# Two short attentions of a four-layer kernel: routing moved into the attention's vector loop, early gathers, output projections unrolled by hand, first loads issued in the projections

## What is computed

```python
# layer 0, mixer: two softmax maps a head, 16 heads of 8
heads = jnp.einsum('bhqk,bhkd->bhqd', w0 - lamb * w1, v).transpose(0, 2, 1, 3)
mu = jnp.mean(heads, axis=-1, keepdims=True)
var = jnp.mean((heads - mu) ** 2, axis=-1, keepdims=True)
normed = (heads - mu) * jax.lax.rsqrt(var + EPS) * ln_w[None, None] + ln_b[None, None]
return jnp.einsum('bse,ed->bsd', normed.reshape(b, s, H * DH), wo)
...
# layer 1, mixer: only the queries with the largest (max - mean) score keep their output
sparsity = scores.max(axis=-1) - scores.mean(axis=-1)
_, top_idx = jax.lax.top_k(sparsity, U)
...
return out @ Wo + bo
...
# layer 1, experts: 64 experts in 8 groups, 8 of a token, from its 4 best groups
scores = jax.nn.sigmoid(logits)
sfc = scores + correction_bias[None, :]
top2, _ = jax.lax.top_k(sfc.reshape(T, G, E // G), 2)
_, gidx = jax.lax.top_k(top2.sum(-1), TOPK_GROUP)
masked = jnp.where(emask > 0, sfc, 0.0)
_, tidx = jax.lax.top_k(masked, K)
tw = jnp.take_along_axis(scores, tidx, axis=1)
tw = tw / (tw.sum(-1, keepdims=True) + 1e-20)          # times 2.5
...
# layer 2, experts: 8 experts of bounded capacity; each token adds the rows of its two
final = jnp.zeros((S + 1, d), xf.dtype).at[idx.reshape(-1)].add(out.reshape(-1, d))[:S]
```

## Time and profile before

| | us |
|---|---|
| median of 3 timed runs | 4274.41 (4273.94 to 4274.72) |
| the profiled execution's own time | 4234.75 |
| its span, first to last instruction | 4232.8 |

### The profile page before, as it was taken

How to read it: one execution, slowest core, us unless ns; L and a number is a source line. 1 busy time by engine, 2 the same in 40 slices (tenths; PEclk the granted TensorE clock), 3 DMA queues, 4 the chain that set the end, 5 groups by cost and what they waited for, 6 DMA issues and landing times. The chain is left out here.

```text
span 4232.8 us, 87140 instructions
## 1 busy us (share of the span) xinstructions
PE 3570.5 (84%) x28212; PEld 2179.9 (52%) x28212; DVE 2473.1 (58%) x5731; ACT 2011.8 (48%) x3955; POOL 1264.9 (30%) x1810
## 2 busy tenths in 40 slices
PE   5799999938997699983299996788987399999997
PEld 2344444426774222222177774357986166666664
DVE  5567777651113577764677776725736366666664
ACT  5366666613334377771033335333334356656662
POOL 0111111100001011110077774423546344444440
PEclk9799999958998699996599997877879599999999
DMA  4322222100001321110266660130003433333330
GB/s 119 80 55 57 57 57 55 39 4 16 11 6 35 77 47 45 42 27 4 63 159 162 159 160 25 71 97 23 3 3 69 66 119 114 111 118 119 114 106 26
DMA packets 198213, 287.69 MB, mean 68 GB/s; under 512 B 40830, under 2 KB 155204, under 8 KB 197624
## 3 DMA queue, kind: packets, MB, share of 16 engines
q1 hardware_dynamic: 193852, 275.81, 23.4%
q0 software_dynamic: 4096, 8.40, 1.4%
HBM read 232.91 MB, written 35.84 MB: 63 GB/s over the span
## 5 line engine op out<-in xcount | busy, mean ns | idle before, releaser
L692 ACT ACTIVATE att_E<-att_pX,att_gs 128x512 f32<-128x512 f32 (+3 forms) x1024 | 722.6, 739 | 400.7 <-PE att_pX L625 176.5
L725 DVE TENSOR_REDUCE att_mx<-att_pS 128x1 f32<-128x512 f32 (+4 forms) x960 | 730.1, 787 | 278.2 <-PE att_pS L599 178.7
L1824 POOL TENSOR_TENSOR att_E<-att_E,att_rz 128x128 f32<-128x128 f32 (+3 forms) x512 | 357.6, 719 | 438.1 <-DVE att_rz L2032 438.1
L594 PE MATMUL att_pS<-att_ks,att_qs 72*128 72x512 bf16 (+4 forms) x1536 | 410.5, 339 | 57.8 <-DMA att_ks<-parts 31.8
L1541 POOL TENSOR_TENSOR pairs_h<-pairs_m,pairs_r 128x512 f32<-128x512 f32 x272 | 345.9, 1272 | 351.2 <-DVE pairs_m L1604 349.7
L619 PE MATMUL att_pX<-att_qs,att_ks 75*128 75x512 bf16 (+4 forms) x1536 | 422.0, 330 | 30.3 <-ACT att_E L692 15.4
L1565 PEld LDWEIGHTS pairs_po<-pairs_a,pairs_h 128*128 128x128 f32 x2176 | 285.9, 192 | 129.6 <-issue 129.1
L556 POOL CAST att_mp<-att_m 16x128 bf16<-16x128 f32 x288 | 80.5, 279 | 900.9 <-DVE att_m L736 875.1
L636 PE MATMUL att_pO<-att_E,att_vs 128*9 128x512 f32 (+3 forms) x3072 | 322.0, 491 | 1.3 <-ACT att_E L692 1.3
L1586 ACT ACTIVATE pairs_r<-pairs_ph 128x512 f32<-128x512 f32 x272 | 162.4, 597 | 330.8 <-PE pairs_ph L1557 330.8
L1963 ACT ACTIVATE att_E<-att_S,att_nm 128x128 f32<-128x128 f32 (+3 forms) x512 | 282.1, 556 | 39.8 <-DVE att_nm L2026 39.6
(11 more groups left out here) (416 smaller groups left out, 6576.6 us busy)
## 6 DMA issues: line engine op xcount, KB each, us to landing
pairs_c<-weights SPq DMA_DIRECT2D x272, 256.0 KB, 3.9
att_bias<-in_bias_dram SPq DMA_DIRECT2D x64, 896.0 KB, 4.6
parts<-proj_part SPq DMA_DIRECT2D x144, 128.0 KB, 2.3
att_xb<-xnT SPq DMA_DIRECT2D x64, 256.0 KB, 2.7
att_qs<-parts SPq DMA_DIRECT2D x192, 64.0 KB
att_ks<-parts SPq DMA_DIRECT2D x192, 64.0 KB
att_w<-in_w3a_dram SPq DMA_DIRECT2D x64, 192.0 KB, 2.4
att_qs<-parts SPq DMA_DIRECT2D x96, 96.0 KB
```

What stands on the lines that cost most here:

```text
L594: ins = nc.tensor.matmul(pS[:, bank, n * w:(n + 1) * w], qs[:K1, u, x, q * P:(q + 1) * P], ks[:K1, u, x, :w], start=(n == 0 or not causal) ...
L692: nc.scalar.activation(E[:, kt % 2, WIDE * xp:WIDE * (xp + 1), :w], places(c)[0], ACT.Exp, scale=gs[:, g % 2, gain_of:gain_of + 1]).then_i ...
L725: V.reduce_max(dst, src, AX.X).then_inc(s_mx, 1)
L1824: nc.gpsimd.tensor_tensor(E[:, k, :width(j)], E[:, k, :width(j)], rz[:, u, k:k + 1].broadcast_to([P, width(j)]), ALU.mult).then_inc(s_n, 1)
```

## The change

Five things are different.

1. The attention's query, key, constant, mask and gain buffers move into a class `Arrivals`, opened around projection and attention. The constants are loaded at the head of the projection's SP queue, and the first group's ten loads in the projection's last body, between the puts of its two sequences. The attention's SP queue begins with group 1.
2. `outproj_phase` is written out for eight sequences. In `out0` the mean is folded into the centring, square, root, transposed copy and result are ACT's, and `ln_w`, `ln_b` are applied by ACT as scale and bias of the transposed copy. DVE centres two sequences ahead. In `out1` one instruction masks a sequence. PE transposes a sequence ahead of the product before. Weights are loaded during the norm.
3. `lg_1` runs before `proj1`, with the sigmoid in its last copy. `route` is no phase any more: its DVE work is cut into 24 steps for four tiles, and DVE's loop in `att1` calls one step at every odd `s`, so that 8 steps stand in each of three groups of four, in each of 8 bodies. Each step begins with a drain. `spread` comes after `att1`.
4. 24 of the 64 gathers are issued by POOL in `recur`, behind items 0, 1 and 2 of each body, into new buffers `rows`; `out2` issues 40.
5. ACT and DVE of `out2` weigh the first two quarters among the gates.

```diff
@@ class Arrivals (new), buffers qs, ks, gains, mb and their semaphores
+    def constants(self, sp):
+        for k, dst in enumerate((self.qs, self.ks)):
+            sp.dma_start(dst[STACK:, :].rearrange("r b x t -> r (b x) t"), self.ext[:, k:k + 1].broadcast_to([self.NX + 3, self.NB * self.UN, T])).then_inc(self.s_ce, 16)
...
@@ project_phase, SP
+                arr.constants(sp)
...
+                        if last and g == M2:
+                            for s in s_put:
+                                sp.wait_ge(s, 24 * M2)
+                            arr.load(sp, 0, 0)
...
@@ attend_phase, DVE
                             for c in PLAN[s]:
                                 if not (last and g + 2 >= NB):
                                     extreme(at, g + 2, c)
+                            if aside is not None and s % 2:
+                                aside(dve, i, g * NP2 // 2 + s // 2)
...
@@ outproj_phase, DVE
+                def center(n):
+                    own = heads[:, n * NH * QT:(n + 1) * NH * QT, :]
+                    V.reduce_sum(mu[:, n % 2], own, AX.X)
+                    dve.drain()
+                    V.scalar_tensor_tensor(out=hc[:, n % 4], in0=wide(mu[:, n % 2]), scalar=-1.0 / DH, in1=own, op0=ALU.mult, op1=ALU.add).then_inc(s_c, 1)
...
+                    center(0)
+                    center(1)
+                    for n in range(B):
+                        variance(n)
+                        if n + 2 < B:
+                            center(n + 2)
+                        scale(n)
...
@@ outproj_phase, PE
+                turn(0)
+                for n in range(B):
+                    if n + 1 < B:
+                        turn(n + 1)
+                    project(n)
...
@@ routing
-    CH = 8
+    CH = 4
...
+        def step(dve, i, k):
+            if k > 23:
+                return
+            dve.drain()
...
+            elif k == 7:
+                V.tensor_tensor(gt[:, :, :, :], each(gs[:, :, :]), other(gs[:, :, :]), ALU.is_gt)
+                V.tensor_tensor(eq[:, :, :, :], each(gs[:, :, :]), other(gs[:, :, :]), ALU.is_equal)
...
@@ recur_phase, POOL
                         ins.then_inc(s_st, 1)
+                        if n < 3:
+                            gather(i * 3 + n)
...
@@ output2_phase, POOL
-                for n in range(NT):
-                    for k in range(2):
-                        nc.gpsimd.indirect_dma_start(rows[k][:, n], None, moe.yout, bass.IndirectOffsetOnAxis(ap=moe.get[:, n, k:k + 1], axis=0)).then_inc(s_get[n // SPAN], 16)
+                for m in range(begun, 2 * NT):
+                    gather(m)
```

More of the change, by code:

```diff
@@ L304, in _, with body @@
             def _(sp):
-                with sp.Fori(0, NBODY) as i:
+                arr.constants(sp)
+                def body(i, first, last):
                     at = At(sp, i)
@@ L510, in load @@
                         sp.wait_ge(s_p2, of(at, NP2, h - NB, NP2))
[L511 to L517, removed]
+                    arr.load(sp, i * NB + h, h % NB)
                 def maxima(at, h):
@@ new lines, in _ @@
+                if norm:
+                    act.wait_ge(s_eps, 1)
+                    act.wait_ge(s_w, loads)
+                    square(0)
+                    square(1)
+                    for n in range(B):
+                        root(n)
+                        if n + 2 < B:
+                            square(n + 2)
+                        if n:
+                            leave(n - 1)
+                        if n >= 2:
+                            result(n - 2)
+                    leave(B - 1)
+                    result(B - 2)
+                    result(B - 1)
+                else:
+                    for n in range(B):
+                        leave(n)
@@ L917, in layer0_attention @@
+                turn(0)
+                for n in range(B):
+                    if n + 1 < B:
+                        turn(n + 1)
+                    project(n)
+def layer0_attention(nc, R, t, early, out):
     with ExitStack() as ctx:
@@ L921, in layer0_attention, with logits_phase @@
         parts = nc.dram_tensor("parts0", (2, B * NH, 2, 3, DH, T), BF16).ap()
-        project_phase(nc, R, "proj0", 4, early, parts, vtok, qscale=True)
-        attend_phase(nc, R, "att0", 2, parts, R.ext0, t["gain0"], vtok, heads, masks=R.masks, lamb=R.lam)
-        outproj_phase(nc, R, "out0", heads, t["wo"], ln=(t["ln_w0"], t["ln_b0"]))
-def logits_phase(nc, R, name, early, NE, lg, xT=None):
+        with phase(nc, "arr0") as p:
+            arr = Arrivals(p, 2, parts, R.ext0, t["gain0"], R.masks)
+            project_phase(nc, R, "proj0", 4, early, parts, vtok, arr, qscale=True)
+            attend_phase(nc, R, "att0", 2, arr, vtok, heads, lamb=R.lam)
+        outproj_phase(nc, R, "out0", heads, out)
+def logits_phase(nc, R, name, early, NE, lg, xT=None, func=ACT.Copy):
     xT = R.xnT if xT is None else xT
@@ L1344, in layer1_attention, with routing @@
         parts = nc.dram_tensor("parts1", (2, B * NH, 1, 3, DH, T), BF16).ap()
[L1345 to L1355 removed]
+        with phase(nc, "arr1") as p:
+            arr = Arrivals(p, 1, parts, R.ext1, t["gain1"])
+            project_phase(nc, R, "proj1", 2, early, parts, vtok, arr, mean={"sum": total})
+            with routing(nc, "route", sc, consts, s_in, comb) as step:
+                attend_phase(nc, R, "att1", 1, arr, vtok, heads, negmax=negmax, aside=step)
+        spread_phase(nc, R, "spread", comb, 64, cT)
+        pick_phase(nc, R, "pick", negmax, total, int(0.6 * 256), mask)
+        outproj_phase(nc, R, "out1", heads, out, mask=mask)
+@contextmanager
+def routing(nc, name, sc, consts, s_in, comb):
+    NE, G = 64, 8
+    CH = 4
+    cb, lo = consts
     with phase(nc, name) as p:
[L1357 to L1358 removed]
         sf = p.sb("sf", [P, CH, NE])
@@ L2810, in _ @@
                     gate(j)
[L2811 to L2813 removed]
+                    if j in (3, 5):
+                        first(j // 2 - 1)
+                for q in range(2, PARTS):
                     first(q)
```

436 lines of the change are left out of this document (207 added, 229 removed).

## The result

The changed kernel takes 4108.99 us (median of 4 runs, 4106.74 to 4112.44) beside 4274.17 us before on the same chip: ratio 0.9617, 95% interval 0.96 to 0.9633, 165 us less. The forecast was 4126, 149 less. On other chips the kernel before takes 4233 to 4239 us and the changed one 4070.52 (ratio 0.9601, 0.9585 to 0.9617): chips differ by 1%, so what follows compares ratios of runs on one chip, and phases of traces. By its time, 4234.75 us, the trace of before in the earlier trace rows comes from one of those faster chips. Where that matters I show the changed kernel run again, on what I call the second chip.

A forecast was written before the change was run, and what follows sets the result against it. PE was taken to pace `att1`, chains through DVE `out0` and `out1`, with PE waiting at `route` and both attention starts, and the end on gathers. Terms summing to -148.7 took the median 4274.4 to 4126; range 4090 to 4168.

The forecast's parts named there:

- out0, -50: `out0`, 84.5 us before, falls to 34.6 with DVE as the bound at 3.45 us a sequence: -50 us.
- Starts of att0 and att1, -5.4 and -5.5: Loads issued during the projections let PE start sooner in `att0` and `att1`: -5.4 and -5.5 us.
- the early loads only move the wait: Rival at the attention starts: SP's queue is full, so the wait only moves; +11 us, 4137; no chance of its own.
- route, -69.8: The `route` phase between `lg_1` and `spread` goes, 71.1 us, less a table load of 1.28 in `lg_1`: -69.8 us.
- Steps, +28: In `att1` the steps bring DVE to 14.15 us a group, 0.5 more than the group: +28 us over 24 groups.
- DVE busy over 95 of 100 us: Sign expected in a 100 us window of `att1`, beside PE about 88 busy and clock 1.00.
- The slower rival, the clock falls in att1: PE's granted clock falls to half in `att1`: +219 us in the place of 28, about 4317; chance 0.03.
- its clock is under 1: Sign that the prediction is wrong: the clock in `att1` is under 1.
- out1, -20: `out1`, 40.5 us before, falls to near 20, with PE going without gaps and its clock rising: -20 us.
- Gathers, -28: 24 fewer gathers in `out2` save 31.5 us and cost `recur` 3: -28 us.
- The worry that DVE and POOL would hold each other up: In `recur`, gathers locked out by DVE operations could take 1.497 us each: 16 us paid instead of 3.
- block ends: Four more blocks or context ends, about 0.6 us each: +2 us.

The follow-up runs named there:

- the run with the loads back: Changed kernel with the first group's ten loads at the head of both attentions again, constants still early; ratio 0.9634 to the kernel before.
- even spreading: Changed kernel with the 24 steps of a body placed six in each of four groups instead of eight in three; ratio 0.9615 to the kernel before.
- dense: Changed kernel with the 24 steps of a body placed sixteen and eight in two groups instead of eight in three; ratio 0.9659 to the kernel before.
- own rows: Changed kernel with a zero row for each dropped token instead of one shared by all; ratio 0.9597 to the kernel before.

## Why the prediction was right, and where it was off

- **out0, -50:** the mechanism held, DVE bound and its five operations a sequence. The term was mis-sized by 4. "A sequence in the steady part: ... = 3.45" measured 3.18, since operations without a dependence overlap by 0.08 us; over six sequences that is 1.6. The tail behind DVE's last scaling (864.82) took 3.4 instead of 5, as the products there took 1.06 us and not 2.1; that is 1.6 more, and the rest is in the first and last sequences.
- **Starts of att0 and att1, -5.4 and -5.5:** -6 to -7 and -6.8. The ten loads were to "push the block's end by 4.05". Against the run with the loads back they push it by 2 to 4 in `proj0`, which is near the forecast; but the rest of the change makes `proj0` shorter by as much (83.9 us with the loads back, 87.1 to 88.3 before), for a reason that no run shows, so that against before nothing is left of the push. SP's queue was not full of its own work: the twelve puts behind the loads go at 0.64 us, not 0.75. In `proj1` (72.1 us with and without the loads) there is no push, where the forecast took 1.3. The rival "the early loads only move the wait" is out: both attentions now wait only for the memset.
- **route, -69.8:** -73.4. The phase's 71.1 us went as taken; `lg_1` did not grow by the table load's 1.28 but lost 2.3 us.
- **Steps, +28:** the size held (31.7), the reason did not. The step that failed is "10.45 + 3.7 = 14.15: 0.5 more than the group. DVE becomes the bound". It describes two groups of four, which take 14.6 and 14.7 us with DVE busy 13.3 and 13.4, but not the price: one stepped group costs nothing, and even spreading, with DVE under the group's time, gains nothing. The forecast's sign, DVE busy over 95 of 100 us, didn't show: it was 86.2. The time behind this term is 22 us in the bodies, half of it the drains, and 10 us by the lower clock, which the sum had at nothing. That 22 and 10 come near to 28 is luck.
- **The slower rival, the clock falls in att1:** its mechanism is there, at 0.03 of chance and 219 us of price. It happened in a small part: 32 us more at the lower level than before, not 24 whole groups. In the dense and even traces PE was at the lower level for 104 and 124 us in all. One of the forecast's signs of being wrong was "its clock is under 1": it is 1.00 in the window of 100 us, but 0.93 over the phase, where before had 0.96. One argument against the rival was a misread row, the next point.
- **out1, -20:** -25.3. The clock rose after the first sequences, as taken (products 1.06 us, a sequence every 1.47). But the reason given, that it had risen in `out1` before, misread: the 1.16 us stand at one product of the first body, and the next six are at half clock again, here the first of them and the window to the end:

```profile
1962.39 2.08 PE L910 MATMUL out_pY<-out_w,out_hT 128*128 128x128 f32 x8 [0.77 <-ACT out_hT L889]
...
1960.00:1988.00 28.00, 18.34 (x72) 15.06 (x72) 9.01 (x28) 3.58 (x6) 0.00 (x0) 0.50 0.00 1
```

So with PE pauses of two us the clock fell back at once; it stayed up in the new order, which leaves none. The rise was foreseen, its ground was not the one given.
- **Gathers, -28:** -26. The worry that DVE and POOL would hold each other up found little: the 24 gathers in `recur` take a median of 995 ns and at most 1107, instead of the 944 taken and the 1497 feared, and `recur` is 3.5 us longer, forecast 3.
- What is left between -148.7 and -163.3 is thus `out1` 5, `out0` 4, `route` with `lg_1` 4, starts 2 to 3, less 4 for the steps and 2 for the gathers, and some 5 in small pieces: the 2 us that I added for block ends don't show, and layer 0's logits are 1.7 us shorter (14.5 to 12.8).

No experiment gave a version that is clear of the changed kernel: own rows are at 0.9597 beside 0.9601, the even steps reach 4060.71 in their best run and 4090.41 in their worst.

## What to carry to other kernels

Work can be hidden in a loop that another engine paces, two thirds of it here. Its price has two parts that need separate runs: one as soon as the steps stand between hand-overs, although the filling engine has time to spare (even: 57.8 us a body instead of 54.7), and one when a group fills that engine (dense: 61.9). Drains are hidden worse than operations: 22 of them cost as much as 32 small operations. And look at the granted clock of the loop that hides the work: every arrangement of the whole steps here brought it down, in amounts that differ between arrangements and between runs of one. Compare ratios on one chip before explaining a difference between a profile and a median.

## What was not expected of the hardware

Gathers whose packets mostly read one shared row hold the DMA engines all of the time (the view gives 1.04) at 107 GB/s; with distinct rows the same rate needs 0.35. Chips differ in this kernel by 1% (4274 and 4234 us), and in the one pair of traces that shows it the excess of the changed kernel lies in three phases of layer 2, while the rest agrees within 4 us.
